# Norm statistics moved to ScalarE and the residual to TensorE, a new row order in the second part, and its first block prepared ahead

## What is computed

```
x = x + mamba(layernorm(x))          # in-projection, conv of 4 taps, silu, 16 recurrent states
                                     #   h_n = exp(A_n dt) h_n + dt B_n x ;  y = sum_n C_n h_n + D x
                                     #   out-projection of silu(y + res)
h = silu(w1 x') * (w2 x')            # x' = layernorm(x), 256 -> 1024
h = gelu(h1 h); h = gelu(h2 h)       # 1024 -> 1024, twice
x = x + w3 h                         # 1024 -> 256
```

## Time and profile before

| | us |
|---|---|
| median of 3 runs (3018.89 to 3022.86) | 3020.08 |
| profiled execution, whole | 3020.71 |
| its span, first to last instruction | 3018.9 |
| part A: first scan at 58.1, last at 2244 | about 2190 |
| end of part A, matmuls only, 2246 to 2316 | 70 |
| part B, first matmul at 2339.1 to the end | 680 |

### The profile page before, as it was taken

One profiled execution on the slowest core, in us unless ns is written; L12 is line 12 of the kernel. 1 busy time (PEld: TensorE's weight loads), 2 busy tenths in 40 slices (PEclk: granted clock), 3 DMA queues, 4 the chain that ended last, 5 costly groups with the idle time before them and its releaser, 6 DMA issues. The chain is left out here.

```text
span 3018.9 us, 49123 instructions
## 1 busy us (share of the span) xinstructions
PE 2677.9 (89%) x17026; PEld 2350.8 (78%) x17026; DVE 2488.2 (82%) x3488; ACT 1831.0 (61%) x3488; POOL 1847.4 (61%) x1549
## 2 busy tenths in 40 slices
PE   5578999999999989999999989999876999999998
PEld 4457888888888878888888888888766787778777
DVE  4999999999999999999999999999962443454434
ACT  4667777777777777777777777777653222222221
POOL 3688888888888888888888888888841000000000
PEclk8799999999999999999999999999988999999999
DMA  6011111211212112211211112121213121222210
GB/s 212 22 50 47 54 54 58 71 61 54 70 55 61 54 54 60 68 61 54 71 54 61 54 54 65 63 61 55 95 66 125 60 82 44 84 84 84 76 51 29
DMA packets 130155, 198.78 MB, mean 66 GB/s; under 512 B 16368, under 2 KB 93296, under 8 KB 129904
## 3 DMA queue, kind: packets, MB, share of 16 engines
q1 hardware_dynamic: 129904, 195.57, 20.7%
HBM read 144.68 MB, written 50.86 MB: 65 GB/s over the span
## 5 line engine op out<-in xcount | busy, mean ns | idle before, releaser
L1107 DVE TENSOR_TENSOR_SCAN h<-banks,ub 128x512 f32<-128x512 f32 x1024 | 1192.1, 1205 | 42.2 <-POOL ub L738 28.9
L738 POOL TENSOR_TENSOR ub<-u,b_row 128x1020 f32<-128x1020 f32 x512 | 1214.0, 2371 | 0.3 <-issue 0.2
L1392 PE MATMUL banks<-ident,h 128*128 128x128 f32 x4096 | 608.8, 280 | 206.0 <-DVE acc L1120 195.4
L954 ACT ACTIVATE banks<-dt,neg_a 128x510 f32<-128x510 f32 x1024 | 683.8, 681 | 142.7 <-DVE h L1107 142.6
L1120 DVE SCALAR_TENSOR_TENSOR acc<-banks,c_tok,acc 128x512 f32<-128x512 f32 x1024 | 714.1, 736 | 5.8 <-PE banks L1392 4.8
L1392 PEld LDWEIGHTS banks<-ident,h 128*128 128x128 f32 x4096 | 473.9, 143 | 294.5 <-issue 126.7
L1380 PE MATMUL banks<-act_high,h_rounded 128*128 128x256 f32 x2048 | 533.3, 297 | 0.0
L1380 PE MATMUL banks<-act_low,h_rounded 128*128 128x256 f32 x2048 | 506.5, 283 | 0.0
L1415 PE MATMUL banks<-act_high,h_rounded 128*128 128x512 f32 x1024 | 419.3, 409 | 71.1 <-DVE act_low L1175 71.1
L1415 PE MATMUL banks<-act_low,h_rounded 128*128 128x512 f32 x1024 | 415.8, 406 | 0.0
L1380 PEld LDWEIGHTS banks<-act_low,h_rounded 128*128 128x128 f32 x2048 | 393.8, 192 | 0.0
(11 more groups left out here) (111 smaller groups left out, 4257.0 us busy)
## 6 DMA issues: line engine op xcount, KB each, us to landing
b_row<-b_scratch SPq DMA_DIRECT2D x128, 512.0 KB, 3.9
z_scratch<-z_out SPq DMA_DIRECT2D x128, 256.0 KB, 5.0
zb<-z_scratch SPq DMA_DIRECT2D x32, 1024.0 KB, 9.0
x_sb<-in_x SPq DMA_DIRECT2D x32, 256.0 KB, 5.4
x_res<-in_x SPq DMA_DIRECT2D x32, 256.0 KB, 4.5
h_full<-in_h SPq DMA_DIRECT2D x2, 4096.0 KB, 17.9
x_scratch<-x_sb SPq DMA_DIRECT2D x32, 256.0 KB, 2.2
xr<-x_scratch SPq DMA_DIRECT2D x16, 512.0 KB, 5.8
```

The source lines that it names most:

```text
L738: nc.gpsimd.tensor_tensor(ub[:, n % 2, :, 1:], u[:, :, 1:], b_row[:, n // QUARTER % 2, n % QUARTER:n % QUARTER + 1, 1:].to_broadcast([P, E ...
L954: nc.scalar.activation(decay_half(k)[:, :, 1:], dt[:, par, 2 * i:2 * i + 2, 1:], ACT.Exp, scale=neg_a[:, n:n + 1]).then_inc(decay_ready, 1)
L1107: nc.vector.tensor_tensor_scan(h[:, n % 2, 2 * i:2 * i + 2].rearrange("p e t -> p (e t)"), banks[:, k % DECAYS, :], ub[:, n % 2, 2 * i:2 * ...
L1392: last = nc.tensor.transpose(turned[q][:, e * P:(e + 1) * P], h[:, n % 2, e, q * P:(q + 1) * P], ident[:])
```

## The change

Part A:
- `bn_stats` and `bn_aggr` leave DVE. ACT's `sums` (place 10) reads each of two row groups with a Copy that also gives their sum, takes minus the mean, and reads them again with a Square (bias minus mean) whose sum gives the variance. The wide outputs go to `xn`, where they are overwritten later.
- `x_res` is added by PE: for each row group one more matmul, the identity times `x_res`, opens the out-projection's accumulation. ACT's `add_rows` (place 20) copies PSUM to `x1_sb` with two Copies that give the sums; `sums2` (place 21) does minus the mean and two Squares. `x1_ready` now comes from ACT.
- The places of several other pieces move by one to four. SP's `load_x` goes from 4 to 1, `write_b` from 8 to 6, the four `read_b` from (12, 14, 2, 7) to (13, 15, 4, 8), `load_res` from 8 to 9; `store_x1` stays at 7.

Part B:
- The first gelu and its split are done in place in three buffers `zl` (the rest takes the place of the input), no longer through `wide`. ACT and DVE take row o of the next block first, then row o of this block. DVE's `finish` moves to behind row 3.
- Block 0: its z is loaded right behind part A's last state; ACT and DVE do its 8 rows within the second body of `ending`; ACT's last table load of part A is that of gelu. PE no longer waits for `pass_a_over`, only for the rounded weights, the added states and its banks. SP loads the z of blocks 1 and 2 once the last h1 group is full. The buffers are laid out anew for this.

```diff
-        DVE_AT = dict(stats=20, x1=26, stats2=32, low2=45, gated=(65, 67, 70, 71, 76, 79, 79, 85))
-        ACT_AT = dict(logs=25, xn=28, xp=(1, 4), conv=(8, 11), silu=11, ssm=17, z=19, soft=22, ...
-        SP_AT = dict(x=4, x1=7, res=8, write_b=8, b=(12, 14, 2, 7), z_out=(40, 41, 51, 53))
+        DVE_AT = dict(low2=45, gated=(64, 67, 70, 72, 76, 79, 80, 85))
+        ACT_AT = dict(sums=10, x1=20, sums2=21, logs=25, xn=31, xp=(1, 3), conv=(8, 11), silu=12, ssm=18, z=19, soft=23, ...
+        SP_AT = dict(x=1, x1=7, res=9, write_b=6, b=(13, 15, 4, 8), z_out=(40, 41, 45, 53))
...
+        FIRST_ROWS = [(CHUNKS + 1, 4 * o) for o in range(KH)]
...
+            def sums(c):
+                act.wait_ge(x_in, 16 * (c + 1))
...
+                for q in range(NT):
+                    last = nc.scalar.activation(xn[:, q], x_sb[:, q], ACT.Copy, accum_out=row_sum[:, q:q + 1])
+                last.then_inc(sum_ready, 1)
+                act.wait_ge(sum_ready, c + 1)
+                nc.scalar.activation(minus_mean[:], row_sum[:], ACT.Copy, scale=-1.0 / DIM).then_inc(mean_ready, 1)
+                act.wait_ge(mean_ready, c + 1)
+                for q in range(NT):
+                    last = nc.scalar.activation(xn[:, q], x_sb[:, q], ACT.Square, bias=minus_mean[:, q:q + 1], accum_out=row_square[:, q:q + 1])
+                last.then_inc(stats_ready, 1)
...
-                    nc.vector.tensor_tensor(x1_sb[:, c % 2].rearrange("p n d -> p (n d)"), bank("out", c), x_res[:].rearrange("p n d -> p (n d)"),
-                                            ALU.add).then_inc(freed("out", c), 1)
+                for q in range(NT):
+                    last = nc.scalar.activation(x1_sb[:, c % 2, q], bank("out", c)[:, q * DIM:(q + 1) * DIM], ACT.Copy, accum_out=row_sum2[:, q:q + 1])
+                last.then_inc(freed("out", c), 1)
...
+                        pe.wait_ge(xres_in, 16 * (c + 1))
+                        nc.tensor.matmul(into[:, q * DIM:(q + 1) * DIM], ident[:], x_res[:, q], start=True, stop=False)
...
                 for blk in range(CB):
                     for o in range(KH):
-                        second(blk, o)
                         if blk + 1 < CB:
                             first(blk + 1, o)
+                        second(blk, o)
...
-                    if blk >= 1:
-                        finish(blk - 1)
                     for o in range(KH):
-                        split_second(blk, o)
                         if blk + 1 < CB:
                             split_first(blk + 1, o)
+                        split_second(blk, o)
+                        if o == W3_AFTER and blk >= 1:
+                            finish(blk - 1)
...
-                pass_a_over(pe)
+                pe.wait_ge(rounded_late, 10)
+                for q in range(NT):
+                    pe.wait_ge(y_added[q], NS * CHUNKS)
```

More of the change, by code:

```diff
@@ L102, in program @@
         ssm = sb("ssm", [P, 2, T], where=a_only)
+        dt = sb("dt", [P, 2, ET, T], where=a_only)
+        u = sb("u", [P, ET, T], where=a_only)
+        b_row = sb("b_row", [P, 2, QUARTER, T], where=a_only)
+        ub = sb("ub", [P, 2, ET, T], where=a_only)
+        h = sb("h", [P, 2, ET, T], where=a_only)
         w_out_sb = sb("w_out_sb", [P, ET, DIM], where=a_only)
@@ L274, in program @@
         PE_AT = dict(
[L275 to L278, removed]
@@ L415, in ending @@
                         post(to_post, n)
[L418 removed]
+                    first_rows(c, n)
+        z_in = [sem(f"z_in{n}") for n in range(3)]
         xr_in = [sem(f"xr_in{n}") for n in range(2)]
         gelu1_ready = sem("gelu1_ready")
[L421 to L422 removed]
+        high1_ready = sem("high1_ready")
+        split1 = sem("split1")
+        high2_ready = sem("high2_ready")
+        split2 = sem("split2")
         e_full = sem("e_full")
@@ L611, in _, with load_z @@
                             sp.dma_start(again[name][:], src.rearrange("(k p) n -> p k n", p=P)).then_inc(late_in, 16)
+            def load_z(blk):
+                for slot in range(2):
+                    sp.wait_ge(z_stored[slot], 16 * PAIRS // 2 * 2 * (blk + 1))
+                for half in range(2):
+                    sp.dma_start(zl[blk % 3][:, :, half * T:(half + 1) * T], z_dram[2 * blk + half]).then_inc(z_in[blk % 3], 16)
+            sp.wait_ge(scan_done, 2 * NS * CHUNKS)
+            for q in range(NT):
+                sp.wait_ge(turn_full[q], NS * CHUNKS)
+            sp.wait_ge(carry_ready, NS * CHUNKS - 2)
+            load_z(0)
             ending(post, mlp, NS)
-            pass_a_over(sp)
             def exact():
[L616 to L619, removed]
                 def load_rows(blk):
@@ L813, in with_logs @@
                     exp_rows2(to_mlp)
-                nc.scalar.preload_act_table_set("exp_and_others")
+                nc.scalar.preload_act_table_set(then)
             def norm(c, n):
+                if n == ACT_AT["sums"]:
+                    sums(c)
                 if n == ACT_AT["logs"] and c < 2:
@@ L1411, in second_layer @@
                     if o == 0:
-                        pe.wait_ge(rows_split, first_row(blk, KH - 1) + 1)
+                        pe.wait_ge(split1, KH * (blk + 1))
                     for k in range(KH):
-                        for part in (act_high, act_low):
-                            last = nc.tensor.matmul(into, rounded["h2"][:, k, o * P:(o + 1) * P], part[:, blk % 2, k],
-                                                    start=(k == 0 and part is act_high), stop=(k == KH - 1 and part is act_low))
+                        for i, part in enumerate((act_high[blk % 2], act_low[blk % 3])):
+                            last = nc.tensor.matmul(into, rounded["h2"][:, k, o * P:(o + 1) * P], part[:, k],
+                                                    start=(k + i == 0), stop=(k == KH - 1 and i == 1))
                     last.then_inc(e_full, 1)
                 def last_layer(blk):
-                    pe.wait_ge(rows_split, second_row(blk, KH - 1) + 1)
+                    pe.wait_ge(split2, KH * (blk + 1))
                     for j in range(NTB // 2):
```

176 lines of the change are left out of this document (92 added, 84 removed).

## The result

The changed kernel takes **2863.84 us** (2863.68 to 2868.78), the kernel before 3021.01 us beside it (3018.89 to 3022.86): a ratio of 0.9488, with a 95% interval from 0.9476 to 0.9500. The profiled execution has a span of 2862.0 us. 2842 us had been predicted, with a range from 2808 to 2890.

A forecast was written before the change was run, and what follows sets the result against it. DVE was taken to set part A's pace, with PE close behind, and PE, not alone, part B's. The terms -73 - 6 + 2 - 22 - 80 = -179 against 3020.7 gave 2842 us, range 2808 to 2890.

The forecast's parts named there:

- Part B's blocks: Part B: the new row order removes the wait at block heads, blocks 36.9 us apart instead of 42.06; -80 us.
- The passage: Between part A's last h1 and part B's first h2 matmul: the 23.4 us gap goes, 1.5 come back; -22 us.
- The last body's reload: Part A's last body: weights reload issued ahead of the third quarter's fetch lands in time; -6 us, bounds -8 and +4.
- Ahead of the bodies: Before part A's bodies: chunk 1's norm statistics now lie on ACT's path; +2 us (0 to 3).
- Clock: Part B: PE's granted clock is 1.00 if PE never stops; a wait of 0.2 us per block is too short to lower it.
- ACT's price: Part A: ACT's added Copies and Squares cost 4.5 us per body (3.0 to 6.2), hidden in its idle time.
- the rival of dear statistics: Part A: statistics on ACT cost 5 us more per body, part A gains nothing; 2915 us, chance 0.04.
- the body's 65.3 us: Part A: one body falls from 67.75 to 65.3 us, bounds 64.2 and 66.8; -73 us over about 30 bodies.
- Both are now equally full: Part A: PE needs 64.0 and DVE 63.9 us per body with short buffers between, so the body can't reach 64.0.
- this coupling: Part A: PE and DVE wait for each other; as a rival, the body keeps 1 of 2.6 us; 2886 us, chance 0.13.
- The fetch of `b_row` behind the store of x1: SP's queue, part A: rows land at 1537.8, POOL starts at 1537.52; called even, 0.3 to 1 us per body included.
- theory 2: Experiments' theory for part A: ACT's stretch with table loads holds state 13's decays, so DVE waits about 1.06 us per body.

The follow-up runs named there:

- the second part alone: The changed kernel with part A put back (DVE takes statistics and addition, old places), part B and the passage left changed: 2917.04 us, ratio 0.9658.
- both places mended: The changed kernel with SP's store of x1 at place 9 instead of 7 and ACT's copy of acc0 at 26 instead of 25: 2852.82 us, ratio 0.9442.
- the copy's place: The changed kernel with ACT's copy of acc0 at place 26, as before the change, instead of 25: 2864.09 us, ratio 0.9483.
- SP's place: The changed kernel with SP's store of x1 at place 9 instead of 7, behind the fetch of b_row's last quarter: 2856.25 us, ratio 0.9451.
- one place moved on ACT: The changed kernel with store of x1 at 9, copy of acc0 at 26, and ACT's third act_high split at 58 instead of 57: 2968.18 us, ratio 0.9824.

## Why the prediction was right, and where not

**Right in size, or within its bounds.** *Part B's blocks*: -80 predicted, -81.5 measured. The 0.2 us of wait that DVE's backlog was to cost in each block didn't come: a block takes 36.77 us. So no run shows whether so short a wait would leave the clock alone, as the prediction took it to. *The passage*: -22, measured -23.4 with 0.7 us lost ahead of it. *The last body's reload*: -6, measured -7.9. *Ahead of the bodies*: +2, measured +0.4. *Clock*: 1.00 where PE no longer stops, as forecast. The restored row order shows that the wait and the slower groups behind it go together.

**ACT's price** was 4.5 us a body, bounds 3.0 to 6.2; measured 54.1 - 50.9 = 3.2. The statistics in ACT's queue:

```profile
1546.12 0.40 ACT L800 ACTIVATE xn<-x_sb 128x256 f32<-128x256 f32 x1
1546.43 0.19 ACT L800 ACTIVATION_READ_ACCUMULATOR xn<-x_sb 128x1 f32 x1
1546.52 0.40 ACT L800 ACTIVATE xn<-x_sb 128x256 f32<-128x256 f32 x1
...
1547.29 0.51 ACT L806 ACTIVATE xn<-x_sb,minus_mean 128x256 f32<-128x256 f32 x1
```

The rule of the Trainium skill ("ScalarE: Activation LUTs", Rules for kernel authors) that such arithmetic belongs on VectorE was the rival of dear statistics. By the single piece of work the rule holds here too: one norm's statistics took VectorE 0.99 us and take ScalarE 2.2 (1546.12 to 1548.29). For the kernel the run of the second part alone shows the opposite: with the statistics and the addition back on VectorE, at the old places, it is 53 us slower. VectorE was the engine that set the pace, ScalarE wasn't.

**The step that failed is the body's 65.3 us**; measured 66.16, so 0.86 x 27 = 23 us, which is about the whole miss of 22 (in full: 73 were forecast for 30 bodies, the 27 and the ends gave 42.4 + 2.9 = 45.3, 28 too little, and the other terms gave some 6 more than forecast). The forecast for DVE was 63.9 us of work and 1.4 of pauses; measured are 64.1 and (500 - 484.83) / 7.56 = 2.0. Of these 2.0 us, 1.06 are the wait for ACT, which the prediction put at nothing because no stretch of ACT was to keep a decay back, 0.50 the wait for POOL, and 0.45 stand under no wait of the list (0.5 before). Three readings failed.

- *The reason given for the loss.* "Both are now equally full": PE needs 62.4 us, not 64.0. The identity's multiplications are there (0.7 us, forecast 0.95), but the others take 1.3 us less; the clock of 1.00 instead of 0.99 would account for about 0.6 of it (an estimate, 1% of 63.0), the rest is open. And PE idles (500 - 471.77) / 7.56 = 3.7 us a body. Leaving the identity's out gained nothing once SP's order was mended. That the 1.4 us put down to this coupling are near the 2.0 measured is luck: none of DVE's listed waits is one for PE.
- *The wait for ACT, missed:* 8.0 / 7.56 = 1.06 us a body. The prediction held each single addition on ACT against the 4.2 us that three banks cover. The stretch that mattered was one that was there already, from DVE's gated product through two table loads to the decays; DVE's statistics at place 32 had been part of its cover, and the change made it 0.5 us longer by the place of the copy. The prediction priced the removal of those statistics at their full length; in the changed kernel, work of 0.87 us at that place costs the body nothing that can be seen.
- *The fetch of `b_row` behind the store of x1, found and half paid.* The times of SP, DMA and POOL were called even, with 0.3 to 1 us included. POOL's wait is 6.9 / 7.56 = 0.9 us a body, and mending it made the body 66.16 - 65.81 = 0.35 us shorter and the run 7.6 us.

What stays open: with both places mended, DVE still waits 4.6 us for ACT and 4.5 for POOL in 500 us. By the trace the way through POOL is the next to shorten; whether a shorter stretch on ACT, with another order of POOL's work behind `dt`, would free both was not tried, so theory 2 is shown as a wait and not as a gain. Nor is the copy's place worth anything that can be seen: by itself it gave 0, and on top of SP's place 3.4 us within overlapping spreads, with equal bodies.

## What to carry to other kernels

Work taken off the full engine is worth its length only where that engine had no wait to come: look, for each instruction removed, at what the engine next needs and when that was ready, above all behind a table load or a fetch. When an engine's order is written by hand, price a moved step by all its readers: one place moved on ACT cost 115 us through POOL, and a store moved ahead of a load cost 7.6. When a run leaves out a piece of work (an ablation) and the kernel gets faster, that does not name the cause; the waits before and after do, and the same run on top of the mended rival settles it. And a wait that shrinks while the time stays has only handed its length to the next one: follow that one back as well.

## What was not expected of the hardware

An accumulator on ACT shows as an instruction of its own, ACTIVATION_READ_ACCUMULATOR, of 0.19 us behind the Copy or Square that fills it (above). It starts before the Copy's end, and the second Copy starts 0.09 us behind it (1546.43 and 1546.52), so its price beside the ACTIVATE is about half of what it shows.

In the tail DVE's subtraction for a split, 0.69 us by the median of 128, once took 1.66 while POOL was in a subtraction of its own:

```profile
2242.81 1.66 DVE L1204 TENSOR_TENSOR act_low<-zl,act_high 128x512 fp32r<-128x512 f32 x1
```

```profile
2242.40 1.53 POOL L778 TENSOR_TENSOR act_low<-wide,act_high 128x512 fp32r<-128x512 f32 x1 [2.66 <-ACT act_high L978]
```

POOL's ended at 2243.93, and DVE's 0.54 us later: DVE had stood nearly until then. The Trainium skill's page "SBUF — State Buffer" (SBUF: two separate sides) says that a VectorE instruction with two SBUF inputs and a GpSimd one that reads SBUF exclude each other for the whole of the one that came first; the trace agrees, by this one pair. POOL's own subtraction took 1.53 us, where its median is 1.29; it began 0.04 us behind a rounding of DVE (at 2242.36, 0.42 us), and whether that held it isn't shown. No other engine waited for DVE's subtraction, and DVE's next instruction waited 0.56 us for ACT all the same, so it cost nothing here.
